# Post-norm attention block with a sign-weight feed-forward on one core: one pool of seven PSUM banks, an earlier projection block, spread row maxima and normalizations

## The reference

```python
qkv = einsum('bsd,ed->bse', x, w_qkv) + b_qkv            # 3 x 16 heads x 32
scores = einsum('bhqd,bhkd->bhqk', q, k) / sqrt(32) + causal
attn = softmax(scores)                                   # over keys
out = einsum('bhqk,bhkd->bhqd', attn, v)
x = layernorm(x + out @ w_out.T + b_out)
hidden = relu((x @ sign(up_weight).T) * up_scale)
x = layernorm(x + (hidden @ sign(down_weight).T) * down_scale * output_scale)
```

## Time and profile before

| what | us |
|---|---|
| three runs | 772.94, 780.11, 778.24 (median 778.24) |
| profiled execution, device time | 774.34 |
| its span, first to last instruction | 772.6 |
| TensorE matmuls busy | 722.7 (94% of the span) |
| VectorE busy | 450.5 (58%) |
| ScalarE busy | 317.2 (41%) |
| GpSimd busy | 354.4 (46%) |
| attention steps 0 to 7, first score to first `up` | 85.4 to 480.5 |

### The profile page before, as it was taken

How to read it: one execution, slowest core, us unless ns; L and a number is a source line. 1 busy time by engine, 2 the same in 40 slices (tenths; PEclk the granted TensorE clock), 3 DMA queues, 4 the chain that set the end, 5 groups by cost and what they waited for, 6 DMA issues and landing times.

```text
span 772.6 us, 11683 instructions
## 1 busy us (share of the span) xinstructions
PE 722.7 (94%) x4032; PEld 505.2 (65%) x4032; DVE 450.5 (58%) x1086; ACT 317.2 (41%) x631; POOL 354.4 (46%) x487
## 2 busy tenths in 40 slices
PE   6899999999999999999979889999999999999993
PEld 4788665655656556565544544788778787878882
DVE  4176495785967859678567751633294339334515
ACT  5211365654655546555546565432232222122210
POOL 4461467394673946739423502632353235223333
PEclk9999999999999999999999999999999999999998
DMA  6976464435544355452677331313012001000101
GB/s 231 296 208 177 110 174 124 136 105 163 150 132 132 108 157 148 115 133 88 174 206 261 109 123 58 120 32 119 14 41 95 28 1 41 15 1 12 44 1 54
DMA packets 44619, 85.71 MB, mean 111 GB/s; under 512 B 4880, under 2 KB 13584, under 8 KB 44432
## 3 DMA queue, kind: packets, MB, share of 16 engines
q1 hardware_dynamic: 35536, 79.72, 34.2%
q10 hardware_dynamic: 9024, 5.24, 2.4%
HBM read 55.33 MB, written 29.36 MB: 110 GB/s over the span
## 4 chain that ended last, share of the span: by engine, by line
PE 71%; DVE 19%; issue 3%; DMA 3%; POOL 2%; ACT 2%; SPq 0%; ACTq 0%; POOLq 0%
PE ps_heads L1045 9%; PE ps_proj L1087 7%; DVE heads_sb L835 7%; PE ps_proj L947 7%; PE ps_score L1104 6%; PE ps_unit L1063 6%; PE ps_unit L1087 5%; PE ps_sum L1039 5%; DVE maxes L813 5%; PE ps_unit L983 4%; PE ps_heads L1104 3%; PE ps_unit L1015 3%; PE ps_sum L1104 3%; PE ps_score L1015 2%; PE ps_score L983 2%
## 5 line engine op out<-in xcount | busy, mean ns | idle before, releaser
L655 POOL TENSOR_TENSOR hid_low<-hid_raw,hid_high 128x512 fp32r<-128x512 f32 x64 | 85.1, 1330 | 175.0 <-DVE hid_high L886 171.9
L711 ACT ACTIVATE probs<-ps_unit 128x512 f32<-128x512 f32 (+3 forms) x216 | 101.9, 490 | 88.4 <-PE ps_unit L1015 85.0
L619 POOL TENSOR_SCALAR_AFFINE_SELECT probs<-probs 128x128 f32<-128x128 f32 x256 | 73.1, 298 | 113.0 <-ACT probs L711 108.9
L711 ACT ACTIVATE probs<-ps_score 128x512 f32<-128x512 f32 (+3 forms) x155 | 75.2, 498 | 77.0 <-PE ps_score L1015 75.6
L886 DVE CAST hid_high<-hid_raw 128x512 fp32r<-128x512 f32 x64 | 27.1, 424 | 125.4 <-ACT hid_raw L766 125.2
L809 DVE CUSTOM_DVE_ANT_0 ps_unit<-ps_unit,causal 128x512 f32<-128x512 f32 (+3 forms) x162 | 80.1, 511 | 32.5 <-PE ps_unit L983 31.5
L1045 PE MATMUL ps_heads<-probs,v_rows 128*32 128x512 f32 (+3 forms) x768 | 80.3, 502 | 11.8 <-DVE heads_sb L837 11.8
L983 PE MATMUL ps_unit<-stack 96*128 96x512 f32 (+3 forms) x246 | 83.8, 354 | 5.7 <-DVE maxes L809 2.5
L1015 PE MATMUL ps_unit<-stack 98*128 98x512 f32 (+2 forms) x216 | 78.4, 366 | 4.1 <-DVE maxes L809 4.0
L613 POOL TENSOR_TENSOR parts<-qk_full,parts 128x512 fp32r<-128x512 f32 x32 | 41.3, 1289 | 64.7 <-ACT parts L690 64.4
L835 DVE RECIPROCAL heads_sb<-ps_sum 128x128 f32<-128x128 f32 x64 | 60.8, 950 | 9.2 <-PE ps_sum L1039 9.2
(11 more groups left out here) (195 smaller groups left out, 1478.0 us busy)
## 6 DMA issues: line engine op xcount, KB each, us to landing
stack<-qk_parts SPq DMA_DIRECT2D x96, 256.0 KB, 4.6
qk_parts<-parts SPq DMA_DIRECT2D x32, 512.0 KB, 2.9
v_all<-h_even ACTq DMA_DIRECT2D x16, 256.0 KB, 3.8
v_rows<-v_all SPq DMA_DIRECT2D x8, 512.0 KB, 4.3
heads_t<-heads_sb SPq DMA_DIRECT2D x16, 256.0 KB, 3.4
raw<-up_w SPq DMA_DIRECT2D x8, 512.0 KB, 3.9
x_tile<-x_rows SPq DMA_DIRECT2D x16, 256.0 KB, 5.5
raw<-down_w SPq DMA_DIRECT2D x8, 512.0 KB, 3.4
```

The lines of the kernel that those rows point to most:

```text
L655: nc.gpsimd.tensor_tensor(hid[1][:, (HM * s + n) % 3, :], hid_raw[:, n % 2, :], hid[0][:, (HM * s + n) % 3, :].bitcast(FP32), ALU.subtract ...
L711: nc.scalar.activation(probs[:, (NP * s + n) % RING, 0:width], bank(what, s, n)[:, off:off + width], ACT.Exp, scale=SCALE).then_inc(s_exp, 1)
```

## The change

- **One pool.** `share()` now gives out seven banks: the five of before, `ps_heads` and `ps_sum`. In steps 0 to 5 each half takes one bank for its heads at its first `pv` and one for its sums at its first sum, and both leave the pool until the entry `back`, which puts them at the end of the order. In step 6 half 0 takes from the five old banks, and from half 1 of step 6 on heads and sums are in `ps_heads` and `ps_sum`. The wait of the first `pv` for the half before is replaced by the wait for the last user of its bank.
- **Spread.** The four `norm` of half 0 are at slots 20.2, 24.3, 28.05 and 32.3, those of half 1 at 52.6, 55, 57.4 and 61.05; `back` is at 36.5 and 65. `MAXIMA` covers slots 0.2 to 43.45. Shift 0 moves from 36.02 to 16, shift 1 from 51.9 to 46.5.
- **Projections one block sooner.** A third block for step 1 is made ahead of step 0, and `BLOCK` gives (1, 3), (2, 0), (2, 1), (2, 2) for all steps. Block k = 2 ends at slot 2.2 and its `stack` is at 9.4.
- **Last steps.** Step 6 is `PAIRED` too, with one block of projections. `fetch` moves from slot 30 of step 6 to 37.5, `split` from 38 to 44 to 45 to 48.6, and `attn`, `y`, `norm1` and `turn` four slots later.
- `w_high` and `w_low`, the parts of the next group's weights, move from slot 19.5 to 13.2.

```diff
-PAIRED_NORM = [19.7, 19.71, 19.72, 19.73, 52.05, 52.06, 52.07, 52.08]
-ALONE = [[11.2, 13.5, 15.7, 18.3, 24, 28, 31.5, 36, 39.5, 43, 46.5, 50.3],
-         [10, 12.4, 15, 17.5, 24, 28, 31.5, 35, 38.5, 42.5, 46, 48.6]]
-ALONE_NORM = [[18.4, 18.41, 18.42, 18.43, 50.4, 50.41, 50.42, 50.43],
-              [17.6, 17.61, 17.62, 17.63, 48.7, 48.71, 48.72, 48.73]]
-MAXIMA = ([11.5 + 0.5 * u for u in range(3)] + [13.4 + 0.48 * u for u in range(13)]
-          + [26.3 + 0.6 * u for u in range(3)] + [28.4 + 0.53 * u for u in range(14)] + [37.5 + 0.66 * u for u in range(15)])
-BLOCK = [(1, 2, 0.5, 0.98, 13.05, 15.8, 18.5), (1, 3, 13.3, 0.5, 19.65, 22.4, 24.8),
-         (2, 0, 20.5, 1.2, 34.4, 37.2, 40), (2, 1, 36.3, 0.6, 44.05, 46.8, 49.2)]
-LAST_BLOCK = [(1, 2, 4.2, 0.48, 9.9, 12.5, 14.9), (1, 3, 11.9, 0.45, 17.1, 19.9, 22.2)]
+PAIRED_NORM = [20.2, 24.3, 28.05, 32.3, 52.6, 55, 57.4, 61.05]
+PAIRED_BACK = [36.5, 65]
+ALONE = [10, 12.4, 15, 17.5, 24, 28, 31.5, 35, 38.5, 42.5, 46, 48.6]
+ALONE_NORM = [17.6, 17.61, 17.62, 17.63, 48.7, 48.71, 48.72, 48.73]
+ALONE_BACK = [23, 54]
+MIXED_NORM = PAIRED_NORM[:4] + [52.05, 52.06, 52.07, 52.08]
+MIXED_BACK = [36.5, 57.9]
+MAXIMA = ([0.2 + 0.7 * u for u in range(6)] + [5.3 + 0.85 * u for u in range(9)] + [13.2 + 1.02 * u for u in range(15)]
+          + [29 + 0.85 * u for u in range(18)])
+BLOCK = [(1, 3, 4.5, 0.69, 13.05, 15.8, 18.5), (2, 0, 20.2, 0.66, 28.05, 30.8, 33.3),
+         (2, 1, 29.5, 0.55, 36.05, 38.8, 41.3), (2, 2, 37, 1.2, 52.1, 54.9, 57.4)]
...
-    for k, at in enumerate((-114, -106)):
+    for k, at in enumerate((-114, -106, -98)):
...
-                put(t + 21.7 + 1.3 * a, "add", s, a)
+                put(t + 21 + 1.9 * a, "add", s, a)
...
-            put(t + 36.02, "shift", s + 1, 0)
-            put(t + 47.2, "row_max", s + 1, 1)
-            put(t + (51.9 if s + 2 < STEPS else 48.2), "shift", s + 1, 1)
+            put(t + 16, "shift", s + 1, 0)
+            put(t + 45, "row_max", s + 1, 1)
+            put(t + 46.5, "shift", s + 1, 1)
...
-        at = NP * (2 * g - 2) + 19.5
+        at = NP * (2 * g - 2) + 13.2
...
+        if what == "pv" and n in (0, FIRST_ADD):
+            f = n // FIRST_ADD
+            take(("heads", s, f), (6,) if s + f >= late else (0, 1, 2, 3, 4, 6, 7)[:5 if s == late - 1 else 7])
+        if what == "sum" and n == 0 or what == "sum_added" or what == "sum" and n == FIRST_ADD:
+            f = 0 if what == "sum" and n == 0 else 1
+            take(("sums", s, f), (7,) if s + f >= late else (0, 1, 2, 3, 4, 6, 7)[:5 if s == late - 1 else 7])
+        if what == "back":
+            order += [users[name, s, n][0] for name in ("heads", "sums")]
...
-                        wait(pe, s_norm, QT * s + 4 * f)
+                        bank_read(users["heads", s, f][1])
+                    if what == "sum" and j == 0:
+                        bank_read(users["sums", s, f][1])
```

More of the change, by code:

```diff
@@ L231, in share, with take @@
 def share(todo):
-    order, had, users = [3, 4, 5, 0, 1, 2], {}, {}
+    order, had, users, late = [3, 4, 6, 7, 5, 0, 1, 2], {}, {}, STEPS - 1
+    def take(user, may):
+        bank = next(k for k in order if k in may)
+        users[user] = bank, had.get(bank)
+        had[bank] = user
+        order.remove(bank)
+        return bank
     for what, s, n in todo:
-        if what not in ("score", "max", "shift"):
-            continue
         if what == "score":
-            may = (2, 3, 4, 5) if s == STEPS - 1 else (0, 1, 2, 3, 4)
-        else:
-            may = (0, 1, 2, 3, 4) if s else (0, 1, 2)
-        bank = next(k for k in order if k in may)
-        users[what, s, n] = bank, had.get(bank)
-        had[bank] = what, s, n
-        order.remove(bank)
-        order.append(bank)
+            order.append(take((what, s, n), (2, 3, 4, 5) if s == late else (0, 1, 2, 3, 4, 6, 7)))
+        if what in ("max", "shift"):
+            order.append(take((what, s, n), (0, 1, 2, 3, 4, 6, 7) if s else (0, 1, 2)))
+        if what == "pv" and n in (0, FIRST_ADD):
[6 more added lines that the diff above has]
+            order += [users[name, s, n][0] for name in ("heads", "sums")]
     return users, had
@@ L431, in bank @@
         def bank(what, s, n):
[L433 removed]
+            return (ps_unit + ps_score + [ps_proj, ps_heads, ps_sum])[users[what, s, n][0]]
         def hidden_used(eng, steps):
@@ L927, in bank_read @@
                     pe.wait_ge(s_ml, 2 * s + n + 1)
+                if what in ("heads", "sums"):
+                    pe.wait_ge(s_norm, QT * s + 4 * n + 4)
             for what, s, n in todo:
@@ L1022, in _ @@
                         pe.wait_ge(s_add, NA * s + NA - GH + h + 1)
-                        nc.tensor.matmul(ps_sum[rows, :], ones[:, :], added[:, h, :], start=True, stop=False,
+                        nc.tensor.matmul(bank("sums", s, 1)[rows, :], ones[:, :], added[:, h, :], start=True, stop=False,
                                          tile_position=(0, h * HD)).then_inc(s_used, 1)
@@ L1038, in _ @@
                         if what == "sum":
-                            nc.tensor.matmul(ps_sum[rows, at:at + width], ones[:, :], tile, **args).then_inc(s_pv, 1)
+                            nc.tensor.matmul(bank("sums", s, f)[rows, at:at + width], ones[:, :], tile, **args).then_inc(s_pv, 1)
                             continue
```

42 lines of the change are left out of this document (22 added, 20 removed).

## The result

The changed kernel takes 808.92 us (median of four runs, 806.43 to 813.91), the kernel before 777.7 on the same chip: a ratio of 1.042, 95% interval 1.038 to 1.047. It is slower by 31 us. The profiled execution took 806.43, its span is 804.7, 32.1 more than before; 2.1 us of that lie ahead of step 0 (the third block), the rest is in the attention steps. From the first `up` to the last matmul both kernels take 280.2 us.

What follows compares the result with a forecast made beforehand. TensorE was the bound, only late starts could be won. Steps 1 to 5 +5.2, step 0 -1.5, step 6 -2.9, step 7 0, a transfer +1: +1.8, giving 776.1 or 780.0; forecast 778.0 us, range 761 to 791.

Steps and rivals of the forecast that it cites:

- Slots 4 to 36 of steps 1 to 5: Regions there would start late by 1.4 to 1.5, 1.9, 0.1 and 0.7 us a step.
- The walk: Region-by-region sum of the new order from earlier prices, not run: late starts 4.5 against 3.7 us a step, +0.8.
- The rest: 0.3: Remaining slots of steps 1 to 5, outside slots 0 to 36: late by 0.3 us a step, before 0.4.
- The cast: Cast of the next weights between units 15 and 16 in steps 2 and 4: adds 0.6 us each.
- Rival B: Boundary of steps 6 and 7: ScalarE holds TensorE over 3 us, clock falls; 788 to 791 us; chance 0.27.
- rows 4 show 1.00 at waits of 0.3: Earlier profile rows with full clock at short waits, set against the clock falling in three-bank regions.
- Step 6: From 55.7 to 50.0 us, -5.7, or -2.9 net of the block made earlier; late starts 13.3, before 15.0.
- Step 0: First step: loses 1.5 us of its late starts; the block made ahead of it costs 2.8 us.
- step 7: Last step: +3 us against -3, so 0; up to 1.5 us of waiting in ScalarE's queue around the splits.
- Block k = 2: Its transfer, needed by unit 16 at slot 14.2, had 0.2 us to spare; 1 us was added for it.
- The sum: All terms together: +0.8 us, or +1.8 with 1 for a transfer.
- The rule on repeated gaps: A repeating gap on the engine that should be saturated can mean too little PSUM; more banks should help everywhere.

Runs made afterwards that it cites:

- e15_queue: The changed kernel with additions and cast at their slots of before and blocks k = 0 and k = 1 moved; 791.53 us, ratio 1.023.
- e3_back: The changed kernel with half 1's normalizations 1.6 slots apart and its banks given back at slot 60.5 instead of 65; 802.96 us, ratio 1.034.
- e1_adds: The changed kernel with the additions back at their slots of before (from 21.7, 1.3 apart); 805.49 us, ratio 1.036.
- e6_block: e1_adds with projection blocks k = 0 and k = 1 also made earlier; 812.04 us, ratio 1.047.
- e5_cast: The changed kernel with only `w_high` and `w_low` back at slot 19.5; 799.98 us, ratio 1.031.
- e10_norms: e9_pool with the normalizations spread and the banks given back at slots 36.5 and 65, as in the change; 790.33 us, ratio 1.019.
- e12_last: e9_pool with the last two steps ordered as in the change; 771.67 us, ratio 0.994.
- e9_pool: The kernel before with all its slots, and only the pool of seven banks added; 771.72 us, ratio 0.995.
- e2_own: The changed kernel with heads and sums in two banks of their own, a pool of five, and normalizations and `back` moved; 833.87 us, ratio 1.072.

## Why the prediction was wrong

The forecast was 778.0 with a range of 761 to 791; it came to 808.9 beside 777.7.

**Bound: right.** TensorE's work in a step didn't change, and all that was lost is late starts and clock.

**Slots 4 to 36 of steps 1 to 5: right.** The walk gave 1.4 to 1.5, 1.9, 0.1 and 0.7 late; measured 1.90, 2.47, 0.20 and 0.83, with the starts late by about 0.1 that the walk had as a term of their own. Cause and place agree: waits for L822 (causal units) ahead of slot 13, a pool of three banks behind it. The forecast of 49.3 us a step, against 49.8 in the kernel where neither GpSimd nor a load nor a copy is waited for (e15_queue), was right to 0.5. e3_back shows the trade that the walk had found.

**"The rest: 0.3": wrong, the step that failed.** The prediction walked TensorE's order and VectorE's and never GpSimd's. The additions were moved to 1.9 slots apart and `high` of two blocks into their midst. That was to be seen from prices of before (1.29 for an addition, the same for a subtraction in GpSimd's timeline): two subtractions, eight additions at 1.29 and the masks are 15.5 us between slots 28.1 and 43.9, while TensorE takes 16.2 there from burst to burst (e15_queue), and the first subtraction can't start before the copy of a block that ends 0.6 slots ahead. It cost 2.2 us between slots 36 and 44 and 0.9 in the burst behind, 3.1 where the prediction had 0.3. Net it is 2.2 a step (52.0 against 49.8, for the blocks of e15_queue take 0.9 elsewhere), 13 in six steps. That it was real, and not always replaced by the next wait, stayed open through e1_adds and e6_block, which put a load and a copy in its place, and was settled by e15_queue.

**The cast: right by itself.** 0.6 for each of steps 2 and 4; 0.5 in step 2, where the clock is the same with and without it (e5_cast). The clock in the same stretch is another matter.

**The clock: right as a mechanism, wrong in its place.** Rival B had it fall once, behind idling of 3 us and more at the boundary of steps 6 and 7. It did not fall there. It was low for 30.6 us more than before (nine times 3.4), most of it from within slots 13 to 19.6 on, and in step 6, where the longest wait is 1.10 us. The sentence that "rows 4 show 1.00 at waits of 0.3" was true and no reason: before, such waits were few. By the price of e10_norms, 1.5 for 3.4 us at 0.50, the 30.6 us more of it are 13.5 us. This is an estimate, for the falls of the change itself weren't taken away one by one. Steps 3 and 5 of the changed kernel agree with it: the same order takes 52.0 at full clock and 54.9 with 6.8 us at 0.50.

**Step 6: wrong, 59.0 for 50.0.** The term for its late starts, 13.3, came to some 22 with the clock in it (59.0 less the 36.7 of work in the prediction's sum). Slots 20 to 28 were put down to VectorE (2.9). What held TensorE there was ScalarE: the signs of the late weights (L730), 1.05 to 1.08 each, stand between the exps, and a bank is free only when its exp is done. TensorE's rows of the changed kernel, and ScalarE's:

```profile
434.59 0.51 PE L998 MATMUL ps_score<-stack 96*128 96x512 f32 x1 [0.69 <-ACT probs L724]
...
437.49 1.81 PE L1065 MATMUL ps_heads<-probs,v_rows 128*32 128x512 f32 x8 [1.10 <-ACT probs L724]
439.06 1.95 PE L1059 MATMUL ps_sum<-probs,ones 128*32 128x512 f32 x8
```

```profile
433.00 1.05 ACT L730 ACTIVATE w_out_high<-raw 128x1024 fp32r<-128x1024 f32 x1
...
435.39 1.08 ACT L730 ACTIVATE w_out_high<-raw 128x1024 fp32r<-128x1024 f32 x1
```

The bursts behind run at the half clock, 1.81 and 1.95 us for eight matmuls that take 1.07 at full clock. e12_last has the same waits in a kernel with before's other steps. Here the old wait did go where the prediction said, but its room was taken by ScalarE. The walk asked which engine is busiest in a region; it should have asked what stands in each queue ahead of the instruction that frees the bank.

**Step 0: wrong, step 7: better.** Step 0 was to get 1.5 shorter. It took 49.3 instead of 45.6, and 46.3 in e1_adds, so 3.0 of it is GpSimd's queue again. The block ahead of it cost 2.1, forecast 2.8. Step 7 is 48.4 instead of 51.1; forecast 0. Of the waiting in ScalarE's queue behind the splits, which the prediction put at up to 1.5, one wait of 1.22 for `probs` came, early in step 7; the rest was won.

**Block k = 2: no wait.** In step 3 its last transfer landed 8.4 after the issue of the store, as the earlier trace rows gave, and the unit didn't wait for it, since slots 4 to 13 were later than in the walk. The 1 us in the sum had no cause.

**The sum.** Span +32.1: ahead of step 0 2.1, step 0 3.7, steps 1 to 5 25.6 (forecast 5.2), step 6 3.3 (forecast -5.7), step 7 -2.7. Read by cause, with overlaps: GpSimd's queue, with the cast and the loads around it, 14.1 (e15_queue); clock about 13.5; what is left is under 5, beside the +1.8 that the prediction had added up. The rule on repeated gaps (the Trainium skill, Perfetto Trace Analysis, Optimization Strategy) turns out half right: with before's order the pool alone gains (e9_pool), and with the spread order it is worth 25 us (e2_own, with the slots that go with it), so more PSUM did help. What the rule has no word on is that the order was changed along with it.

## What to carry to other kernels

Walk every in-order queue that a moved instruction enters, with the prices of the profile before, also one that is idle for half of the time: load between two deadlines counts, and so does an instruction in its midst that waits for another engine. Allow for the clock behind many short waits in a row: in e10_norms it added 1.5 us to their 2.3 in each of five steps, while in steps 1 and 3 of the changed kernel it added nothing. In a pool of banks given out in turn, what counts is who held the bank last and how far its reader is behind: moving six units by 0.2 to 1.1 slots gave 10 us, where spreading everything had lost 31.
